# Two graph layers over 400,000 sorted edges: tiles of 126 edges in place of 125, 127 batches in place of 128

## The reference, cut to what matters

```python
# layer 0 (spline): 9 basis weights per edge, 32 x 32 matrices
row, col = (edge_index[0], edge_index[1])
basis = _basis(pseudo)
messages = jnp.einsum('ek,ei,kio->eo', basis, x[row], weight)
out = jnp.zeros((x.shape[0], weight.shape[2]), dtype=x.dtype).at[col].add(messages)
...
# layer 1 (tensor): a small network of the distance gives 384 numbers per edge
R = jax.nn.relu(abs_distances[:, None] @ w1 + b1) @ w2 + b2
Y = spherical_harmonics(rel_vec)
Fj = features[src]
...
acc = acc + _NORM[i] * jnp.einsum('euv,ef,evi,ofi->euo', Rb[..., k], Yf, Fb, C)
...
out = out.at[dst].add(msg)
```

## Time and profile before

| what | us |
|---|---|
| runs shown, median | 9837.15 (9836.03 to 9838.02, 3 runs) |
| the profiled execution, its own time | 9820.02 |
| its span, first to last instruction | 9818.2 |
| mean granted clock of PE over the span | 0.838 |
| layer 0, first gather to end of the last | 3.82 to 4848.29 |
| layer 1, first gather to end of the last | 4908.26 to 9764.26 |

### The profile page before, as it was taken

How to read it: one execution, slowest core, us unless ns; L and a number is a source line. 1 busy time by engine, 2 the same in 40 slices (tenths; PEclk the granted TensorE clock), 3 DMA queues, 4 the chain that set the end, 5 groups by cost and what they waited for, 6 DMA issues and landing times. The chain is left out here.

```text
span 9818.2 us, 126393 instructions
## 1 busy us (share of the span) xinstructions
PE 7058.8 (72%) x31138; PEld 3614.5 (37%) x31138; DVE 6056.4 (62%) x15302; ACT 2782.2 (28%) x6973; POOL 7750.6 (79%) x6407
## 2 busy tenths in 40 slices
PE   6555555555555555555588888888888888888888
PEld 3222222222222222222344444444444444444444
DVE  4443434344444434444488888888888888888887
ACT  1000000000000000000144444444444444444443
POOL 7777777777777777777677777787777777777786
PEclk7777677676767677777699999999999999999999
DMA  2111111111111111111122222222222222222222
GB/s 29 14 14 14 14 14 14 14 14 14 14 14 14 14 14 14 14 14 14 31 55 55 53 54 54 54 54 54 54 54 54 52 56 53 55 52 56 52 55 49
DMA packets 738237, 338.75 MB, mean 35 GB/s; under 512 B 655759, under 2 KB 672074, under 8 KB 737964
## 3 DMA queue, kind: packets, MB, share of 16 engines
q0 software_dynamic: 307200, 212.25, 13.2%
q10 hardware_dynamic: 20480, 102.42, 4.1%
q1 hardware_dynamic: 410537, 23.86, 2.9%
HBM read 324.64 MB, written 6.40 MB: 34 GB/s over the span
## 5 line engine op out<-in xcount | busy, mean ns | idle before, releaser
L170 POOL DMA_INDIRECT rows<-table_dram,idx_a x1920 | 2324.7, 1211 | 645.0 <-issue 640.1
L170 POOL DMA_INDIRECT rows<-in_x,idx_a x1920 | 2321.6, 1209 | 587.3 <-issue 587.3
L595 PE MATMUL sums_all<-shared 125*64 125x289 f32 x6400 | 2066.6, 518 | 692.2 <-issue 691.0
L472 DVE TENSOR_TENSOR shared<-own_ps,rows 125x1440 f32<-125x1440 f32 x640 | 1059.9, 1656 | 2333.0 <-DMA rows<-in_x,idx_b 1380.1
L170 POOL DMA_INDIRECT rows<-table_dram,idx_b x1280 | 1556.0, 1216 | 390.3 <-issue 385.7
L170 POOL DMA_INDIRECT rows<-in_x,idx_b x1280 | 1547.4, 1209 | 390.3 <-issue 390.3
L904 PE MATMUL sums_ps<-prods,hot 125*64 125x272 f32 x12800 | 1652.6, 405 | 185.6 <-issue 163.1
L595 PEld LDWEIGHTS sums_all<-shared 125*64 125x64 f32 x6400 | 985.3, 174 | 1589.5 <-issue 1262.0
L682 ACT ACTIVATE flat<-sums_all 64x289 f32<-64x289 f32 x640 | 261.4, 408 | 4369.6 <-PE sums_all L595 4110.9
L894 PE MATMUL radial_x<-w2p,hidden 128*125 128x384 f32 x3840 | 1410.5, 504 | 34.4 <-ACT hidden L859 34.2
L614 PE MATMUL msg_ps<-sums,wk 96*33 96x320 f32 (+1 forms) x768 | 432.6, 734 | 1359.7 <-DVE acc L481 1359.7
(11 more groups left out here) (149 smaller groups left out, 5421.6 us busy)
## 6 DMA issues: line engine op xcount, KB each, us to landing
dist_ab<-in_edge_weight ACTq DMA_DIRECT2D x128, 468.8 KB
dist_ab<-in_edge_weight ACTq DMA_DIRECT2D x128, 312.5 KB
rows<-in_x,idx_a POOLq DMA_INDIRECT x1920
rows<-table_dram,idx_a POOLq DMA_INDIRECT x1920
rows<-in_x,idx_b POOLq DMA_INDIRECT x1280
rows<-table_dram,idx_b POOLq DMA_INDIRECT x1280
vec_s<-in_edge_attr SPq DMA_DIRECT2D x129, 36.6 KB
idx_a<-in_src SPq DMA_DIRECT2D x257, 7.3 KB
```

Of the source, the lines that this page charges most:

```text
L170: pool.indirect_dma_start(out=rows[u][:, j, 0:width], out_offset=None, in_=table, in_offset=bass.IndirectOffsetOnAxis(ap=idx[u // 3][:, u ...
L472: dve.tensor_tensor(spread[s][:, :, 0:K].rearrange("e t (k c) -> e t k c", c=C), basis[s].unsqueeze(3).to_broadcast([EP, G, 9, C]), rows[u ...
L595: last = pe.matmul(sums_ps[s][:, 0:K + 1], hot[s][:, j, :], spread[s][:, j, :], start=(j == 0), stop=(j == G - 1))
```

## The change

The tile has 126 edges, so that a unit has 630 and a batch 3150. 127 batches would hold 400,050 edges, 50 too many: the last batch starts at edge 396,850, 50 edges early, and so repeats the last 50 of the batch before. For these 50 (the first ten partitions of its first unit) `rel_t` is set to -1, which matches none of the window's columns. As the start of the last batch is no multiple, it can't come from a loop register: the last but one batch is written out too wherever it loads or prepares the last. `dst_i` is loaded in two DMAs, 126 batches and the last. In layer 1 PE, POOL and DVE keep their loops.

```diff
-EP = 125
+EP = 126
-T = E // EP
...
-B = T // (G * U)
-TPP = 25
-PL = T // TPP
+TPP = G * U
+B = -(-E // (TPP * EP))
+T = B * TPP
+PL = B
...
 EDGES = G * EP
+TWICE = B * U * EDGES - E
+
+
+def batch_start(i):
+
+    return E - U * EDGES if isinstance(i, int) and i == B - 1 else i * (U * EDGES)
...
-    part = array[bass.ds(i * (U * EDGES) + u0 * EDGES, n * EDGES)]
+    part = array[bass.ds(batch_start(i) + u0 * EDGES, n * EDGES)]
...
-            by_batch = dst.rearrange("(p f) -> p f", p=PL)
+            by_batch = dst[0:(B - 1) * U * EDGES].rearrange("(p f) -> p f", p=B - 1)
+            last_batch = dst[E - U * EDGES:E].rearrange("(p f) -> p f", p=1)
...
-            sp.dma_start(dst_i[:, :], by_batch[:, :]).then_inc(dst_landed, 16)
+            sp.dma_start(dst_i[0:B - 1, :], by_batch[:, :]).then_inc(dst_landed, 16)
+            sp.dma_start(dst_i[B - 1:B, :], last_batch[:, :]).then_inc(dst_landed, 16)
...
-                with sp.Fori(0, B - 1) as i:
+                with sp.Fori(0, B - 2) as i:
                     body(i, i + 1)
+                body(B - 2, B - 1)
                 body(B - 1, 0)
...
-            dve.wait_ge(dst_landed, 16)
+            dve.wait_ge(dst_landed, 32)
...
                 chain(dve.tensor_scalar(pos, pos, 2.0, -1.0, ALU.mult, ALU.add), 2)
+                if isinstance(i, int) and i == B - 1:
+                    for u in range(-(-TWICE // EDGES)):
+                        dve.memset(rel_t[0:min(EP, (TWICE - u * EDGES) // G), i * UG + u * G:i * UG + (u + 1) * G], -1.0)
...
-                with dve.Fori(ADD_LAG, B - 1) as i:
+                with dve.Fori(ADD_LAG, B - 2) as i:
                     body(i, True, False)
+                body(B - 2, True, False)
                 body(B - 1, True, True)
```

More of the change, by code:

```diff
@@ L113 @@
 EDGES = G * EP
+TWICE = B * U * EDGES - E
+def batch_start(i):
+    return E - U * EDGES if isinstance(i, int) and i == B - 1 else i * (U * EDGES)
 def unit_edges(array, i, u0, n):
-    part = array[bass.ds(i * (U * EDGES) + u0 * EDGES, n * EDGES)]
+    part = array[bass.ds(batch_start(i) + u0 * EDGES, n * EDGES)]
     return part.rearrange("(u p j) -> p u j", u=n, j=G)
 def unit_vectors(array, i, n):
-    part = array[bass.ds(i * (U * EDGES), U * EDGES)]
+    part = array[bass.ds(batch_start(i), U * EDGES)]
     return part.rearrange("(u p j) c -> p u (j c)", u=U, j=G)
@@ L788, in load_dist @@
             u0, u1 = DIST[h]
-            part = edge_weight[bass.ds(i * (U * EDGES) + u0 * EDGES, (u1 - u0) * EDGES)]
+            part = edge_weight[bass.ds(batch_start(i) + u0 * EDGES, (u1 - u0) * EDGES)]
             eng.dma_start(dist_ab[HID * h:HID * (h + 1), 0:(u1 - u0) * EDGES],
@@ L871, in body @@
                             load_dist(act, after, h)
-                with act.Fori(0, B - 1) as i:
+                with act.Fori(0, B - 2) as i:
                     body(i, i + 1)
+                body(B - 2, B - 1)
                 body(B - 1, 0)
```

## The result

The changed kernel took 10,838.24 us (median of 4 runs, 10,818.73 to 10,849.7), the kernel before, beside it, 9837.58 us (4 runs, 9836.03 to 9838.22). The ratio is 1.1015 [1.0996, 1.1034]: 10% slower. The forecast was 8370 us, and the result lies outside its range.

What follows compares the result with a forecast made beforehand. POOL's gathers, one every 1.51 us, were taken as the bound. Span 3.8 + 3908 + 60.0 + 29 + 4308 + 38.3 + 5 = 8352, plus 1.8 + 17.1, gave 8370 us; range 7550 to 9775.

Steps and rivals of the forecast that it cites:

- Part (1): Batches 128 to 127: 25 gathers fewer in each layer, 76 us off POOL's path.
- The split of a gather: DMA engines sharing a gather's rows equally: 5 for 125 rows (26 rounds), 14 for 126 (10 rounds).
- One reading of the prediction: Layer 1 gather on q0: 64 packets read as 48 + 16, because 9600 B have to be cut in three.
- Rival A: POOL's gather time is fixed at 1.21 us, so only the fewer batches count: 9761 us; chance 0.22.
- Part (4): Layer 1: PE ends last at 6.785 us a unit once a gather takes under 1.357 us; 4308 us.
- rival B: Layer 1 goes at DVE's pace, 6.15 us a unit, not PE's: 7970 us; chance 0.07.
- Part (6): The start: after filling five buffers, POOL waits some 5 us once for the first product; +5.
- Part (3): Layer 0: POOL stays the bound, five gathers 6.15 us against DVE's 3.1 and PE's 4.3 us a unit.
- Part (2): POOL's slots per gather: ten rounds give 0.93 us a gather, 1.23 with the issue gap; layer 0 3908 us.
- the midpoint taken: Fixed part of POOL's gather time, set midway between 0.29 and 1.21 us: 0.75 us.
- the estimate of 8600 us: Whole-kernel time if POOL's gather takes 1.30 us with its gap, from the skill's about 1 us emission.
- rival D: Real rows on more DMA engines cost POOL time, making gathers dearer: 10,810 us; chance 0.04.

Runs made afterwards that it cites:

- occasions 1, 3, 4 and 5: Follow-up measurements beside the kernel before, which took 9826.23, 9817.90, 9817.60 and 9819.05 us; kernels with cheap gathers took 8388 to 8565 us.
- 125-row run: Changed kernel with gathers fetching 125 of the 126 rows, the 126th edge's row left as zeros: 9749.53 us, ratio 0.9927 to the kernel before.
- 96-row kernel: Kernel before with gathers of 96 of 125 rows, the rest zeros: 8389.11 us; with the last but one batch written out, 11,120.68 us in another measurement.
- occasion 4: Follow-up measurement with the change itself run again unaltered: 8561.47 us, ratio 0.8721 to the kernel before beside it, 9817.60 us.
- first measurement: The changed kernel's original timing, 10,838.24 us, beside the kernel before, 9837.58 us; ratio 1.1015.
- slow occasions: Measurements where the kernel before took 9838 us or more and kernels with cheap gathers took 10,838 to 11,121 us.
- quick occasions: Measurements where the kernel before took 9818 to 9826 us and kernels with cheap gathers took 8388 to 8565 us.
- 3149 ones: Changed kernel with batches starting 3149 edges apart, no batch written out, no memset, for timing alone: 8564.86 us, ratio 0.872; in another measurement 11,075.10 us.

## Why the prediction was wrong

**What held.** On occasions 1, 3, 4 and 5 the steps can be checked one by one.

- Part (1), 76 us: 76.7 measured.
- The split of a gather, 5 engines for 125 rows and 14 for 126: shown by the surplus of 136 B, and by the 125-row run. One reading of the prediction is not explained by its reason: the 64 packets of a gather in layer 1 fit only if the 11 engines without rows also send three each, and 9600 B are no reason for them. Where the Trainium skill ("DMA: Bandwidth & Descriptors", section on the semaphore increment of 16) gives the largest divisor up to 16, the trace agrees with 14 now too.
- Rival A, the fixed gather: refuted. It gave 9761; only the 125-row kernel came out there, 9749.53. The sentence of the Trainium skill that spoke for it (same page, breakdown of the fixed cost: many descriptors before the incremental cost shows) doesn't hold here: 16 rounds fewer (0.997 against 1.209 us) go with 0.21 us less.
- Part (4), PE's unit of 6.785 us: layer 1 passes 737 gathers in 1000 us, 1000 x 5/737 = 6.784 us a unit, at a granted clock of 1.00. The 96-row kernel passes 737 as well, with a gather of 0.92 us: PE is the bound and rival B (DVE's pace) is refuted. POOL's wait for DVE was forecast as hundreds of microseconds. The profile names DVE for 5.5 us alone, but POOL is held back once in five gathers all the same, with the gap put down to "issue" (0.60 us in the line below, 0.30 otherwise): 4296.5 us for 3175 gathers, about 170 more than at 1.30 us each. That is little because 1.30 us lies just under PE's 1.357. With the gather of 0.92 us the gap is 0.9 to 1.0 us and the profile does name DVE's products, 568.9 us.

```profile
7009.14 1.00 POOL L176 DMA_INDIRECT rows<-table_dram,idx_a  x1 [0.60 <-issue]
```

- Part (6), the start: POOL waits once, 4.9 us, for L484; forecast 5.
- Part (3): POOL stays the bound of layer 0, 770 gathers in 1000 us, waiting for "issue" alone but for those 4.9 us. DVE's wait for gathered rows at the product fell from 2333 to 1835 us, 498 where 900 were forecast. Some 220 of the missing 400 us are the dearer gather (below), and another 136 came off DVE's wait for `vec_s` instead (202.9 to 67.4).

**A term mis-sized.** Part (2): 0.93 us was taken, 0.997 came. The fixed part is not 0.75: with (1.209 - 0.997)/16 = 13.2 ns a round it would be 0.865. In layer 0, 3175 x 1.30 = 4127 us is 219 more than the 3908 of the sum. The sum with 1.30 us per gather is 3.8 + 4127 + 60 + 29 + 4308 + 38.3 + 5 = 8571 us of span; measured on occasion 4: 8558.7. The Trainium skill's 1 us for such an emission (same page, section on latency) was nearer than the midpoint taken, and so was the estimate of 8600 us worked out from it.

**The step that failed.** Parts (3) and (4) ask "what is next" when POOL gets faster, and take the engines' own work from the trace of before, as if PE and SP would go on issuing as they do there. In the first measurement they didn't. Part (4) gave PE 6.785 us a unit; in the window 7000 to 8000 a unit took 5000/549 = 9.1 us. Part (3) left POOL the bound of layer 0; POOL waited 747 us there for DVE, and DVE for PE. Against occasion 4, the same code:

- layer 0, first gather to the end of the last: 4855.5 us against 4131.8, 724 more;
- between the layers: 72 against 57;
- layer 1, first gather to the end of the span: 5885.9 against 4366.2, 1520 more.

Together 2258 us, the difference of the spans (10,816.9 less 8558.7). In layer 0 the sums of L608 come one matmul at a time; ACT's copies of them (`flat`, L695) and DVE's basis (L476) wait for them, then POOL. In layer 1 each hole of PE stops DVE (1003 us until PE's drain at line 910, against 343 on occasion 4) and through it POOL (1707.8 us). The lower granted clock, 0.67 and 0.89 against 0.75 and 1.00, adds to it: `radial_y` takes 623 ns a matmul on average against 510. Two thirds of the loss, 1520 of 2258 us, is layer 1's, where SP's long register operations are almost absent; that the holes there have the same origin as the one-by-one stretches of layer 0 is inferred from their coming and going together.

The forecast gave 4% to slower, and for one mechanism only: rival D, a gather made dearer by more real addresses, at 10,810 us. The number is close to 10,838 by chance. Its mechanism is refuted: the gather takes 1.00 us in the slow trace as in the quick one.

**What stays open.** What the circumstance of the slow occasions is. The runs show that it touches the kernel before by at most 1% (9911 against 9818) and every kernel with cheap gathers by 27 to 33% (10,838 and 11,068 against 8561; 11,121 against 8388). Whether it is the quicker pace of the gathers, or that they use 14 or 16 DMA engines in place of 5, that gives it its hold was not separated. The kernel before, with 5 engines and the old pace together, ran on the slow occasions and lost 1% at most, but was not traced there; the change with 125-row gathers wasn't run on one, nor a gather on 14 or 16 engines slowed down. Nor was it tested whether other work on the machine, or the single chip behind a number, makes an occasion slow. PE and SP (DVE too, in the 96-row kernel) on a grid of 0.70 us look like engines served in turn by one server, each instruction brought singly; that is inference. The trace's two queues of kind "instruction" carry the same 8 and 13 packets in both traces and show nothing of it. The Trainium skill ("Runtime: NRT & Kernel Launch", section on instruction fetch mechanics) says that a taken branch breaks the sequential prefetch of instructions when its target lies outside the window of pages at hand; the loops do branch, but they do so on quick occasions too, so no run here shows that rule at work.

**Which version is best.** The 96-row kernels and the 3149 ones leave edges out. Of the two kernels that compute everything, the change is 13% quicker than the kernel before on occasion 4, and by its 3149 form, which stands in for it, on three more; on three it is 10 to 12% slower (on one of these again by the 3149 form); a choice between it and the kernel before depends on how often each occurs, and seven occasions don't tell that well.

## What to carry to other kernels

In these runs an indirect gather's time on POOL fell with the slots that its equal shares need per DMA engine (1.209, 0.997 and 0.921 us): choose a number of rows with a large divisor up to 16 (126 or 96, not 125), and read the surplus of bytes on its queue to see the split. When an engine that paced everything gets faster, the trace of before cannot show how the others issue under the new load; a change of this kind is to be timed on several occasions, each beside the kernel before, and its control must run on the same occasion. If a page shows "issue" with no engine full, count the sequencers' register operations of about 700 ns on every engine. One line is not enough (37 ns in the slow 96-row kernel), nor is one stretch (26 of 702 in layer 1, which lost most).

## What the runs showed that was not expected

- The same program took 8561, 10,838 and 11,068 us on different occasions, each repeated within 0.3%, with the same instructions and packets. In stretches PE and SP started one instruction per multiple of about 0.70 us; POOL's gathers kept their 1.30 us wherever they did not wait for DVE.
- The price of a gather is not a straight line in rounds: 13.2 ns a round from 26 to 10, but 25 ns from 10 to 7 (0.997 to 0.921), where 30 real rows go as well. A price of 1.2 ns per row besides 13.3 per round would fit all three (0.71 us fixed), but three points don't test three numbers.
- The packets' time on q0 hardly differs between slow and quick occasions. For the change it is 952 us (8.8% of 10,817) and 1085 (9.8% of 11,067) on slow ones against 1087 (12.7% of 8559); for the 3149 kernel 1162 (10.5% of 11,067) against 1147 (13.4% of 8559). The gathers' own transfers are not what is slow.
